# Head attention of a decoder: key chunks in three rounded passes, spread queries fetched in two halves

## The chip, the cores and the metric

The kernel runs on one core of one Trainium2 chip. The metric is the device time of one execution in microseconds. The engines are TensorE (PE, whose weight loads are shown as PEld), VectorE (DVE), ScalarE (ACT) and GpSimd (POOL); SyncE (SP) issues the DMAs.

## What is computed

A decoder of two layers over 32 batches of 56 tokens of width 128. Each layer has a self-attention, a cross-attention on a context of 1500 rows a batch, and a mixture of experts. The part that matters here is the cross-attention of the second layer, with 16 heads of width 8:

```python
def _L1_xattn_ref(query, key, value, Wq, bq, Wk, bk, Wv, bv, Wo, bo):
    q = proj(query, Wq, bq)      # x @ W.T + b, split into 16 heads
    k = proj(key, Wk, bk)
    v = proj(value, Wv, bv)
    scores = jnp.einsum('bhqd,bhkd->bhqk', q, k) / jnp.sqrt(jnp.float32(D_K))
    attn = jax.nn.softmax(scores, axis=-1)
    ctx = jnp.einsum('bhqk,bhkd->bhqd', attn, v)
    ctx = ctx.transpose(0, 2, 1, 3).reshape(B, Sq, D_MODEL)
    return ctx @ Wo.T + bo
...
x = x + _L1_xattn_ref(_layernorm(x, axis=-1), ctx_1024, ctx_1024, ...)
```

## The kernel before

The program runs seven stages one after the other; `head_attention` (from line 1490) is the sixth. Activations are held transposed, channels on partitions. The context of batch p, transposed to 128x1500, comes by one DMA into `ct[u]`, u = p mod 2 (`load`, line 1539).

For each batch the stage makes:

- **Keys.** Three chunks of 500 columns, each one f32 matmul of `HWkT` with a chunk of `ct` into bank 7 (`some_keys`, line 1644). ACT adds the bias and writes `kf` (`copy_keys`, line 1741); GpSimd rounds it to `kh` (line 1799) and subtracts for the remainder `kl` (line 1801), both in the rounded type fp32r. Twelve DMAs (line 1567) place `kh`, `kl`, `kh` below one another in `k3`.
- **Values.** Twelve tiles in three groups of four, f32 (`values`, line 1634), copied to `vs` by ACT (line 1735).
- **Peaks.** 21 matmuls in the rounded type (`peak`, line 1604), numbered m = 0 to 20, into banks 4 and 5 in turn. DVE takes each one's maximum (line 1853). Matmul m waits for maximum m - 2. The maxima's own maximum is turned by TensorE (line 1688) and written to row 96 and on of `q3` (line 1869), as the softmax's shift.
- **Scores.** Twelve tiles t of 125 keys (`score`, line 1623), from `k3` and `q3`; the latter is spread by GpSimd out of `qs` (line 1785, four instructions), which holds the queries and their remainders. ACT takes each tile's exponential (line 1728). Score t waits for exponential t - 2.
- **Weighing.** Twelve tiles of f32 matmuls (`weigh`, line 1614) sum the weighted values in bank 6. DVE picks the sums (`pick`, lines 1825 to 1830), TensorE sums the weights (lines 1589 and 1590), ACT makes the inverse by a logarithm and an exponential (`invert`, lines 1721 and 1723), and DVE multiplies (`divide`, line 1836, whose inputs `on` and `rc` both lie in SBUF).

A slot p holds keys of batch p, peaks and values of p - 1, scores of p - 2, the last four weighings and the pick of p - 3, and the inverse and the divide of p - 4. Every engine has its own written list for a slot, in three rounds i = 0, 1, 2, and works through it strictly in order; semaphores (`Flow.wait`) tie the lists together. `staged` (line 1880) writes slots 0 to 3 out, runs slots 4 to 31 in a loop of two at a time, with addresses in registers, and writes slots 32 and 33 out. In round 0 the lists run:

- TensorE: peak 0, score 0, peak 1, score 1, peak 2, sum of weights, peak 3, weighings 8 to 11 of p - 3, peak 4, score 2, peak 5, values 0, peak 6, score 3, peak 7, values 1.
- ACT: exponentials 0 and 1, `invert`, exponential 2, values, exponential 3, values.
- DVE: maxima 0 to 3, `divide`, `pick`, maxima 4 to 7.
- GpSimd: the spreading of the queries, then `qm` (line 1790, needed by the next slot's peaks), then the rounding of each key chunk as it comes.

In round 1 come scores 4 to 7, peaks 8 to 15, values 2 and, after peak 14, key chunk 0; in round 2 scores 8 to 11, peaks 16 to 20, key chunk 1 after peak 18, the turned maxima, and key chunk 2 between scores 10 and 11. At the start of the stage `spread_queries` (line 1551) fetches all 32 batches' queries into `qs` with 12 DMAs, in SyncE's list before the keys of slot 1. GpSimd waits with the first spreading for all of them.

Of the kernel before, what the change touches and what calls it, by code (L numbers as in the profile page):

```python
# [14 lines left out]
NT = B * L  # L15
# [1474 lines left out]
def head_attention(g):  # L1490
# [13 lines left out]
    with ExitStack() as ctx:  # L1504
# [4 lines left out]
        kf, kl = sb("kf", [128, S]), sb("kl", [128, S], F32R)  # L1509
        kh = [sb(f"kh{u}", [128, S], F32R) for u in range(2)]  # L1510
# [3 lines left out]
        qs = sb("qs", [96, G, NT])  # L1514
# [26 lines left out]
        with nc.Block() as block:  # L1541
            @block.sync
            def _(sp):
                def spread_queries():
                    for n, part in enumerate((g.xn, g.xn, ql)):
# [7 lines left out]
                def slot(p, u, h, keys, maxima, sums):  # L1553
# [17 lines left out]
                staged(sp, B, slot)  # L1571

            @block.tensor
            def _(pe):
# [71 lines left out]
                def slot(p, u, h, keys, maxima, sums):  # L1646
# [56 lines left out]
                staged(pe, B, slot)  # L1703
# [7 lines left out]
            def _(act):  # L1711
                give(act, v_copied, k_full, exped, logged, inverted)
# [24 lines left out]

                def copy_keys(p, n):
# [4 lines left out]
                def slot(p, u, h, keys, maxima, sums):  # L1743
# [21 lines left out]
                staged(act, B, slot)  # L1765
# [4 lines left out]
            def _(pool):  # L1770
                give(pool, q_spread, qm_made, k_high, k_low)
# [6 lines left out]
                def slot(p, u, h, keys, maxima, sums):  # L1778
# [459 lines left out]
```

## Time and profile before

| | us |
|---|---|
| time, median of 3 runs | 1679.98 (1679.1 to 1684.31) |
| time of the profiled execution | 1683.96 |
| its span | 1682.2 |
| head attention in it | about 687 to 1451 |
| TensorE busy, whole span | 1544.6 (92%) |
| DVE busy | 1129.9 (67%) |
| ACT busy | 881.1 (52%) |
| GpSimd busy | 726.3 (43%) |

Times in the trace are microseconds from the start of the span; L1604 is line 1604. A row of the timeline merges instructions of one line that follow each other closely: it shows the first start, the time to the last end and the count. Matmuls are pipelined: the distance from one start to the next tells what one costs, not its recorded duration. The f32 matmuls have two records each.

### The profile page before, as it was taken

The page shows a single profiled execution, that of the slowest core. Times are in us where ns is not written, and L with a number is a line of the kernel's source. Part 1 is how long each engine was busy: PE and PEld are TensorE (multiplying, and loading weights), DVE is VectorE, ACT ScalarE, POOL GpSimd, SP SyncE. Part 2 cuts the span into 40 slices and gives each one's busy share as a digit, 9 for nine tenths or more (in the row PEclk, how much of TensorE's full clock was granted, in tenths as well). Part 3 has the DMA queues.
Part 4 walks back from the last instruction along what each step waited for, and adds up shares of the span by engine and source line. Part 5 has one row for each costly group of instructions (what it writes and reads, how often), then busy time and mean ns, then how long its engine had stood idle before and what let it go on. Part 6 is the DMA issues. An engine that isn't in the chain of part 4 may idle for free. (4 is left out here: it accounts for less than half of the span.)

```text
span 1682.2 us, 45110 instructions
## 1 busy us (share of the span) xinstructions
PE 1544.6 (92%) x16354; PEld 1198.6 (71%) x16354; DVE 1129.9 (67%) x1760; ACT 881.1 (52%) x1387; POOL 726.3 (43%) x786
## 2 busy tenths in 40 slices
PE   7988999899999867679999999999999999889997
PEld 3544766689999545357777777777777777578886
DVE  3643555667887467467777777777777777267877
ACT  4453332432222345436666666666666666566664
POOL 0200000577877444534444433444444333267775
PEclk8988999999999888789999999999999999989999
DMA  2018994131100000286555556665555565112211
GB/s 74 1 34 208 261 255 123 39 124 63 52 30 23 0 2 1 70 180 142 135 132 133 130 137 146 146 146 128 133 132 132 132 146 110 39 36 70 69 56 44
DMA packets 53115, 168.83 MB, mean 100 GB/s; under 512 B 12592, under 2 KB 24720, under 8 KB 53040
## 3 DMA queue, kind: packets, MB, share of 16 engines
q1 hardware_dynamic: 50880, 156.30, 37.2%
q10 hardware_dynamic: 2160, 11.52, 2.4%
q8 instruction: 48, 0.79, 0.2%
q14 instruction: 27, 0.22, 0.0%
HBM read 90.27 MB, written 1.03 MB: 54 GB/s over the span
## 5 line engine op out<-in xcount | busy, mean ns | idle before, releaser
L1853 DVE TENSOR_REDUCE hat_tops<-banks 128x1 f32<-128x500 f32 x672 | 441.7, 677 | 157.9 <-PE banks L1604 156.5
L1728 ACT ACTIVATE hat_pb<-banks 125x896 f32<-125x896 f32 x384 | 340.2, 916 | 226.0 <-PE banks L1623 221.6
L1604 PE MATMUL banks<-hat_kh,hat_qm 128*128 128x500 f32 x672 | 299.4, 463 | 8.2 <-issue 4.8
L1623 PEld LDWEIGHTS banks<-hat_q,hat_k 128*125 128x125 f32 x1536 | 220.3, 189 | 70.9 <-ACT hat_pb L1728 31.9
L1623 PE MATMUL banks<-hat_q,hat_k 128*125 128x224 f32 x1536 | 250.9, 286 | 12.8 <-ACT hat_pb L1728 9.2
L1799 POOL CAST hat_kh<-hat_kf 128x500 fp32r<-128x500 f32 x96 | 58.6, 610 | 391.5 <-DMA hat_k<-hat_kh 303.6
L1614 PE MATMUL banks<-hat_pb,hat_vs 125*27 125x168 f32 (+1 forms) x6144 | 166.9, 261 | 0.1
L1614 PEld LDWEIGHTS banks<-hat_pb,hat_vs 125*27 125x27 f32 (+1 forms) x6144 | 132.0, 98 | 44.1 <-issue 24.4
L1604 PEld LDWEIGHTS banks<-hat_kh,hat_qm 128*128 128x128 f32 x672 | 128.7, 193 | 45.0 <-DVE hat_tops L1853 25.4
L1186 ACT ACTIVATE ffn_rg<-banks 128x448 f32<-128x448 f32 x128 | 69.9, 546 | 162.6 <-PE banks L1120 162.4
L2091 DVE TENSOR_TENSOR moe_hl<-moe_hf,moe_hh 128x448 fp32r<-128x448 f32 x128 | 121.3, 981 | 37.3 <-POOL moe_hh L1982 32.2
L2068 ACT ACTIVATE moe_hf<-banks,moe_b 128x448 f32<-128x448 f32 x144 | 91.6, 637 | 66.1 <-PE banks L2008 55.0
L1801 POOL TENSOR_TENSOR hat_kl<-hat_kf,hat_kh 128x500 fp32r<-128x500 f32 x96 | 120.7, 1257 | 7.7
L1091 POOL CAST ffn_hh<-ffn_hf 128x448 fp32r<-128x448 f32 x112 | 91.1, 813 | 51.4 <-DVE ffn_hf L1232 51.4
L1232 DVE TENSOR_TENSOR ffn_hf<-ffn_rg,banks 128x448 f32<-128x448 f32 x128 | 78.9, 617 | 47.5 <-ACT ffn_rg L1186 45.8
L1634 PE MATMUL banks<-w_HWvT,hat_ct 128*125 128x128 f32 x768 | 103.6, 279 | 0.1
L1634 PEld LDWEIGHTS banks<-w_HWvT,hat_ct 128*125 128x125 f32 x768 | 98.3, 191 | 7.1 <-ACT hat_vs L1735 2.9
L894 POOL CAST ffn_wh<-ffn_raw 128x512 fp32r<-128x512 f32 x24 | 15.4, 641 | 203.9 <-DMA ffn_raw<-FWdT 203.9
L1118 PE MATMUL banks<-n_xh,ffn_wh 128*128 128x448 f32 x256 | 95.0, 371 | 7.3 <-DVE ffn_hf L1232 5.7
L1644 PE MATMUL banks<-hat_ct,w_HWkT 128*128 128x500 f32 x192 | 97.0, 587 | 3.7 <-ACT hat_kf L1741 3.7
L1203 DVE TENSOR_TENSOR ffn_hl<-ffn_hf,ffn_hh 128x448 fp32r<-128x448 f32 x113 | 92.2, 816 | 4.2 <-POOL ffn_hh L1091 4.2
L1120 PE MATMUL banks<-n_xl,ffn_wh 128*128 128x448 f32 x256 | 93.6, 366 | 0.0
(280 smaller groups left out, 3088.7 us busy)
## 6 DMA issues: line engine op xcount, KB each, us to landing
hat_k<-hat_kh SPq DMA_DIRECT2D x256, 187.5 KB, 4.8
hat_ct<-ctxT SPq DMA_DIRECT2D x32, 750.0 KB, 6.1
hat_k<-hat_kl SPq DMA_DIRECT2D x128, 187.5 KB, 4.4
ctx_cx<-ctx SPq DMA_DIRECT2D x32, 672.0 KB
ctx_cd<-ctxT ACTq DMA_DIRECT2D x15, 750.0 KB, 5.9
ffn_cb<-expert_weights SPq DMA_DIRECT2D x8, 896.0 KB, 4.4
moe_cb<-expert_weights SPq DMA_DIRECT2D x8, 896.0 KB, 6.5
moe_raw<-Mw SPq DMA_DIRECT2D x18, 256.0 KB, 3.0
```

The lines of the kernel that those rows point to most:

```text
L1118: nc.tensor.matmul(out, a_high, b_high, start=start, stop=False, skip_group_check=True)
L1120: return nc.tensor.matmul(out, a_high, b_low, start=False, stop=stop, skip_group_check=True)
L1203: low.inc(v.tensor_tensor(hl[:, j % 4, :], hf[:, j % 4, :], hh[:, j % 4, :].bitcast(F32), ALU.subtract))
L1604: peak_out.inc(nc.tensor.matmul(g.bank(PK + m % 2)[:, 0:SB], qm[u][:].rearrange("p h i -> p (h i)")[:, r * 128:r * 128 + 128], kh[u][:, c ...
L1614: mm = nc.tensor.matmul(g.bank(PV)[32 * j:32 * j + V9 * w, n * L:(n + w) * L], vs[u][:, t, HG * j + n:HG * j + n + w, :].rearrange("p h e ...
L1623: mm = nc.tensor.matmul(g.bank(2 * (t % 2) + j // 2)[0:SW, (j % 2) * QW:(j % 2 + 1) * QW], k3[u][:, j, t * SW:(t + 1) * SW], q3[u][:, j, : ...
L1634: mm = nc.tensor.matmul(g.bank(MISC)[0:SW, (i % 4) * D:(i % 4 + 1) * D], ct[u][:, i * SW:(i + 1) * SW], g.w["HWvT"][:], start=True, stop=True)
L1644: k_out.inc(nc.tensor.matmul(g.bank(MISC)[:, 0:SB], g.w["HWkT"][:], ct[u][:, n * SB:(n + 1) * SB], start=True, stop=True))
L1728: exped.inc(nc.scalar.activation(pb[t % 6][:].rearrange("p (n i) -> p n i", n=2), g.ps[0:SW, 2 * (t % 2):2 * (t % 2) + 2, 0:2 * QW], ACT.E ...
L1801: k_low.inc(nc.gpsimd.tensor_tensor(kl[:, cols], kf[:, cols], kh[u][:, cols].bitcast(F32), ALU.subtract))
L1853: peaked.inc(v.tensor_reduce(tops[:, r, n:n + 1], g.bank(PK + m % 2)[:, 0:SB], AX_X, ALU.max))
L2091: low.inc(v.tensor_tensor(hl[:, j % 8, :], hf[:, j % 8, :], hh[:, j % 8, :].bitcast(F32), ALU.subtract))
```

## The change

- Each key chunk becomes three matmuls in the rounded type, which add up in the same bank: high weights with high context, low weights with high context, high weights with low context.
- The weights are split once, at the start of the stage: ACT copies the high part to `kwh`, GpSimd subtracts for `kwl`.
- The context is split in every slot, three chunks of 500 columns: ACT copies (`round_context`) to `cth`, GpSimd subtracts for `ctl`. In ACT's list chunk 0 lies between exponentials 0 and 1, chunk 1 between exponential 1 and `invert`, chunk 2 between exponentials 4 and 5. In GpSimd's list the three subtractions lie between the spreading of the queries and `qm`. `round_context` waits for the context's load, which TensorE's key matmul did before.
- `qs` holds 16 batches in place of 32. The 12 DMAs are issued twice, with half the bytes: in slot 1 and in slot 16, there after the keys' DMAs and once the spreading of batch 15 is done. GpSimd waits for the second set in slot 17.
- `staged_halves` takes the place of `staged` in this stage: slots 4 to 15 in a loop, 16 to 19 written out, 20 to 31 in a loop. In the second half the column in `qs` is counted from batch 16 (`late`).

```diff
@@ tiles
+        cth, ctl = sb("cth", [128, S], F32R), sb("ctl", [128, S], F32R)
+        kwh, kwl = sb("kwh", [128, 128], F32R), sb("kwl", [128, 128], F32R)
+        c_high, c_low = flow("c_high", 3), flow("c_low", 3)
-        qs = sb("qs", [96, G, NT])
+        qs = sb("qs", [96, G, NT // 2])
@@ SyncE
-                def spread_queries():
+                def spread_queries(half):
+                    cols = slice(half * (NT // 2), (half + 1) * (NT // 2))
...
-                            sp.dma_start(qs[32 * n:32 * n + 32, j, :], part[32 * j:32 * j + 32, :]).then_inc(q_in, 16)
+                            sp.dma_start(qs[32 * n:32 * n + 32, j, :], part[32 * j:32 * j + 32, cols]).then_inc(q_in, 16)
...
                     if isinstance(p, int) and p == 1:
-                        spread_queries()
+                        spread_queries(0)
...
+                    if isinstance(p, int) and p == B // 2:
+                        q_spread.wait(sp, p - 1)
+                        spread_queries(1)
@@ TensorE
                 def some_keys(p, u, h, n):
                     if n == 0:
-                        pe.wait_ge(loaded[u], 16 * h + 16)
                         v_copied.wait(pe, p - 1)
+                        if isinstance(p, int) and p == 0:
+                            pe.wait_ge(kw_low, 1)
                     else:
                         k_full.wait(pe, p, n)
-                    k_out.inc(nc.tensor.matmul(g.bank(MISC)[:, 0:SB], g.w["HWkT"][:], ct[u][:, n * SB:(n + 1) * SB], start=True, stop=True))
+                    c_low.wait(pe, p, n + 1)
+                    cols = slice(n * SB, (n + 1) * SB)
+                    nc.tensor.matmul(g.bank(MISC)[:, 0:SB], kwh[:], cth[:, cols], start=True, stop=False)
+                    nc.tensor.matmul(g.bank(MISC)[:, 0:SB], kwl[:], cth[:, cols], start=False, stop=False)
+                    k_out.inc(nc.tensor.matmul(g.bank(MISC)[:, 0:SB], kwh[:], ctl[:, cols], start=False, stop=True))
@@ ACT
+                nc.scalar.copy(kwh[:], g.w["HWkT"][:]).then_inc(kw_high, 1)
...
+                def round_context(p, u, h, n):
+                    if n == 0:
+                        act.wait_ge(loaded[u], 16 * h + 16)
+                    k_out.wait(act, p - 1, n + 1)
+                    cols = slice(n * SB, (n + 1) * SB)
+                    c_high.inc(nc.scalar.copy(cth[:, cols], ct[u][:, cols]))
...
                     for i in range(IT):
                         if sums:
                             exponential(p - 2, 4 * i)
+                        if i == 0 and keys:
+                            round_context(p, u, h, 0)
+                        if i == 1 and keys:
+                            round_context(p, u, h, 2)
+                        if sums:
                             exponential(p - 2, 4 * i + 1)
+                        if i == 0 and keys:
+                            round_context(p, u, h, 1)
                         if i == 0 and reached(p, 4):
                             invert(p - 4)
@@ GpSimd
+                pool.wait_ge(kw_high, 1)
+                nc.gpsimd.tensor_tensor(kwl[:], g.w["HWkT"][:], kwh[:].bitcast(F32), ALU.subtract).then_inc(kw_low, 1)
...
+                        if isinstance(p, int) and p == B // 2 + 1:
+                            pool.wait_ge(q_in, 24 * 16)
...
                     if keys:
+                        for n in range(3):
+                            cols = slice(n * SB, (n + 1) * SB)
+                            c_high.wait(pool, p, n + 1)
+                            c_low.inc(nc.gpsimd.tensor_tensor(ctl[:, cols], ct[u][:, cols], cth[:, cols].bitcast(F32), ALU.subtract))
                         peak_out.wait(pool, p - 2)
                         qm_made.inc(nc.gpsimd.tensor_tensor(qm[u][:], ...
@@ the order of the slots
+def staged_halves(engine, n, slot):
+    for p in range(4):
+        slot(p, p % 2, p // 2, True, p >= 1, p >= 2)
+    with engine.Fori(0, n // 4 - 2) as turn:
+        slot(turn * 2 + 4, 0, turn + 2, True, True, True)
+        slot(turn * 2 + 5, 1, turn + 2, True, True, True)
+    for p in (n // 2, n // 2 + 1, n // 2 + 2, n // 2 + 3):
+        slot(p, p % 2, p // 2, True, True, True, p > n // 2)
+    with engine.Fori(0, n // 4 - 2) as turn:
+        slot(turn * 2 + (n // 2 + 4), 0, turn + (n // 4 + 2), True, True, True, True)
+        slot(turn * 2 + (n // 2 + 5), 1, turn + (n // 4 + 2), True, True, True, True)
+    slot(n, 0, n // 2, False, True, True, True)
+    slot(n + 1, 1, n // 2, False, False, True, True)
```

## Rows read from the trace of the kernel before

**Rows 1.** Windows: length; busy PE, PEld, DVE, ACT, POOL; PEclk, DMA share, GB/s.

```profile
...
770.00:1400.00 630.00, 620.09 (x8390) 492.37 (x8390) 474.83 (x759) 412.25 (x562) 260.90 (x308) 1.00 0.59 138
...
```

**Rows 2.** Timeline, ACT, slots 31 and 32: start, duration, instruction, idle before.

```profile
...
1387.14 2.62 ACT L1728 ACTIVATE hat_pb<-banks 125x896 f32<-125x896 f32 x3
...
1389.95 0.30 ACT L1723 ACTIVATE hat_rc<-hat_rc 128x112 f32<-128x112 f32 x1
...
1400.61 0.92 ACT L1728 ACTIVATE hat_pb<-banks 125x896 f32<-125x896 f32 x1 [2.39 <-PE banks L1623]
...
1408.08 0.92 ACT L1728 ACTIVATE hat_pb<-banks 125x896 f32<-125x896 f32 x1 [2.29 <-PE banks L1623]
1408.92 0.68 ACT L1741 ACTIVATE hat_kf<-banks,w_Hbk 128x500 f32<-128x500 f32 x1
1409.50 2.61 ACT L1728 ACTIVATE hat_pb<-banks 125x896 f32<-125x896 f32 x3
...
```

**Rows 3.** Timeline, TensorE, same columns, slots 31 and 32.

```profile
...
1393.10 0.48 PE L1604 MATMUL banks<-hat_kh,hat_qm 128*128 128x500 f32 x1
...
1400.41 0.39 PE L1604 MATMUL banks<-hat_kh,hat_qm 128*128 128x500 f32 x1
...
1401.70 0.59 PE L1623 MATMUL banks<-hat_q,hat_k 128*125 128x224 f32 x4
...
1403.84 0.40 PE L1604 MATMUL banks<-hat_kh,hat_qm 128*128 128x500 f32 x1
...
1405.46 1.74 PE L1614 MATMUL banks<-hat_pb,hat_vs 125*27 125x168 f32 x64
...
1425.73 0.62 PE L1604 MATMUL banks<-hat_kh,hat_qm 128*128 128x500 f32 x2
...
1427.31 1.74 PE L1614 MATMUL banks<-hat_pb,hat_vs 125*27 125x168 f32 x64
...
```

**Rows 4.** Timeline, DVE, slots 31 and 32.

```profile
...
1390.46 1.10 DVE L1836 TENSOR_TENSOR spare<-hat_on,hat_rc 128x112 f32 x1
...
1392.30 2.65 DVE L1853 TENSOR_REDUCE hat_tops<-banks 128x1 f32<-128x500 f32 x4
...
1412.81 0.59 DVE L1836 TENSOR_TENSOR spare<-hat_on,hat_rc 128x112 f32<-128x112 f32 x1
...
```

**Rows 5.** Timeline, TensorE, expert stage, two passes in a row.

```profile
...
1565.39 0.37 PE L2007 MATMUL banks<-moe_hh,moe_wl 128*128 128x448 f32 x1
1565.59 0.37 PE L2008 MATMUL banks<-moe_hl,moe_wh 128*128 128x448 f32 x1
...
```

**Rows 6.** Source view, line 1716: min/median/max ns, first and last start.

```profile
...
L1716 ACT CAST spare<-xn x4: 564/564/565, 705.7 to 707.5; 128x448 fp32r<-128x448 f32 x4
...
```

**Rows 7.** Timeline, GpSimd, slots 31 and 32, single spreadings among them.

```profile
...
1388.10 1.26 POOL L1801 TENSOR_TENSOR hat_kl<-hat_kf,hat_kh 128x500 fp32r<-128x500 f32 x1
...
1390.87 0.56 POOL L1785 TENSOR_TENSOR hat_q<-hat_qs,constants 96x224 fp32r<-96x224 f32 x1
1391.39 1.72 POOL L1790 TENSOR_TENSOR hat_qm<-xn,constants 128x896 fp32r<-128x896 f32 x1
1402.75 0.60 POOL L1799 CAST hat_kh<-hat_kf 128x500 fp32r<-128x500 f32 x1 [9.64 <-DMA hat_k<-hat_kh]
...
1412.70 0.56 POOL L1785 TENSOR_TENSOR hat_q<-hat_qs,constants 96x224 fp32r<-96x224 f32 x1
...
```

**Rows 8.** Timeline, GpSimd and DVE, start of the stage.

```profile
...
707.59 1.94 POOL L1790 TENSOR_TENSOR hat_qm<-xn,constants 128x896 fp32r<-128x896 f32 x1 [8.38 <-issue]
...
707.90 2.11 DVE L1821 TENSOR_TENSOR spare<-xn,spare 128x448 f32<-128x448 f32 x1
...
```

**Rows 9.** Timeline, TensorE, start of slot 2.

```profile
...
735.95 0.76 PE L1604 MATMUL banks<-hat_kh,hat_qm 128*128 128x500 f32 x1 [4.78 <-issue]
...
```

**Rows 10.** SyncE: key DMAs, slot 31; line 1539, context loads, us to landing.

```profile
...
1395.00 2.79 SPq L1567 DMA_DIRECT2D hat_k<-hat_kh  x4
...
DMA to landing us min/median/max: 4.3/6.1/9.3
...
```

More of the change, by code:

```diff
@@ L1509, in head_attention @@
         kf, kl = sb("kf", [128, S]), sb("kl", [128, S], F32R)
+        cth, ctl = sb("cth", [128, S], F32R), sb("ctl", [128, S], F32R)
+        kwh, kwl = sb("kwh", [128, 128], F32R), sb("kwl", [128, 128], F32R)
+        c_high, c_low = flow("c_high", 3), flow("c_low", 3)
+        kw_high, kw_low = sem("kw_high"), sem("kw_low")
         kh = [sb(f"kh{u}", [128, S], F32R) for u in range(2)]
@@ L1550, in spread_queries, with slot @@
                         for j in range(G):
-                            sp.dma_start(qs[32 * n:32 * n + 32, j, :], part[32 * j:32 * j + 32, :]).then_inc(q_in, 16)
-                def slot(p, u, h, keys, maxima, sums):
+                            sp.dma_start(qs[32 * n:32 * n + 32, j, :], part[32 * j:32 * j + 32, cols]).then_inc(q_in, 16)
+                def slot(p, u, h, keys, maxima, sums, late=False):
                     if keys and (not isinstance(p, int) or p >= 2):
@@ L1639, in some_keys, with slot @@
                     if n == 0:
-                        pe.wait_ge(loaded[u], 16 * h + 16)
                         v_copied.wait(pe, p - 1)
+                        if isinstance(p, int) and p == 0:
+                            pe.wait_ge(kw_low, 1)
                     else:
                         k_full.wait(pe, p, n)
-                    k_out.inc(nc.tensor.matmul(g.bank(MISC)[:, 0:SB], g.w["HWkT"][:], ct[u][:, n * SB:(n + 1) * SB], start=True, stop=True))
-                def slot(p, u, h, keys, maxima, sums):
+                    c_low.wait(pe, p, n + 1)
[3 more added lines that the diff above has]
+                    k_out.inc(nc.tensor.matmul(g.bank(MISC)[:, 0:SB], kwh[:], ctl[:, cols], start=False, stop=True))
+                def slot(p, u, h, keys, maxima, sums, late=False):
                     for i in range(IT):
@@ L1702, in _ @@
                 pe.wait_ge(norm.logged, CH)
-                staged(pe, B, slot)
+                staged_halves(pe, B, slot)
                 for t in range(ST - 4, ST):
@@ L1711, in _ @@
             def _(act):
-                give(act, v_copied, k_full, exped, logged, inverted)
+                give(act, v_copied, k_full, exped, logged, inverted, c_high)
+                nc.scalar.copy(kwh[:], g.w["HWkT"][:]).then_inc(kw_high, 1)
                 norm.on_act(act)
@@ L1741, in copy_keys, with slot @@
                     k_full.inc(nc.scalar.activation(kf[:, n * SB:(n + 1) * SB], g.bank(MISC)[:, 0:SB], ACT.Identity, bias=g.w["Hbk"][:, 0:1]))
-                def slot(p, u, h, keys, maxima, sums):
+                def slot(p, u, h, keys, maxima, sums, late=False):
                     for i in range(IT):
@@ L1763, in slot @@
                             copy_values(p - 1, 1 - u, 1)
-                staged(act, B, slot)
+                staged_halves(act, B, slot)
                 invert(B - 2)
@@ L1770, in _ @@
             def _(pool):
-                give(pool, q_spread, qm_made, k_high, k_low)
+                give(pool, q_spread, qm_made, k_high, k_low, c_low)
+                pool.wait_ge(kw_high, 1)
+                nc.gpsimd.tensor_tensor(kwl[:], g.w["HWkT"][:], kwh[:].bitcast(F32), ALU.subtract).then_inc(kw_low, 1)
+                pool.wait_ge(kw_low, 1)
                 for u in range(2):
@@ L1776, in _, with slot @@
                 pool.wait_ge(q_full, CH)
-                def slot(p, u, h, keys, maxima, sums):
+                def slot(p, u, h, keys, maxima, sums, late=False):
                     if maxima:
@@ L1801, in slot @@
                             k_low.inc(nc.gpsimd.tensor_tensor(kl[:, cols], kf[:, cols], kh[u][:, cols].bitcast(F32), ALU.subtract))
-                staged(pool, B, slot)
+                staged_halves(pool, B, slot)
             @block.vector
@@ L1834, in divide @@
                         dve.wait_ge(q_in, 12 * 16)
+                    if isinstance(q, int) and q == B // 2 - 2:
+                        dve.wait_ge(q_in, 24 * 16)
                     inverted.wait(dve, q)
@@ L1838, in _, with slot @@
                 give(dve, peaked, topped, shifted, own, picked, normed)
-                def slot(p, u, h, keys, maxima, sums):
+                def slot(p, u, h, keys, maxima, sums, late=False):
                     for i in range(IT):
@@ L1871, in slot @@
                                                     spread(c_["own_chunk"][96:96 + ROWS, 0:ROWS], 2, 128), ALU.mult))
-                staged(dve, B, slot)
+                staged_halves(dve, B, slot)
                 divide(B - 2)
```

4 lines of the change are left out of this document (2 added, 2 removed).

## The prediction

> **What bounds the kernel now.** I began with the page's busy shares, then took the window view of the stretch that the change touches, the steady part of the head attention. From 770 to 1400 us TensorE (PE) is busy 620.09 of 630 us at a granted clock of 1.00, DVE 474.83, ACT 412.25 and GpSimd (POOL) 260.90 [rows 1]. So PE sets the pace and each other engine is idle a quarter of the time or more. Idle time, though, is only useful where it lies, so I laid out one slot (one batch's turn of the pipeline) engine by engine. I count from the start of the exponential of tile 11 on ACT, the last of slot 30, at 1387.14 us, into slot 31; the next one is at 1409.50 [rows 2], so a slot is 22.36 us. There are 28 slots with the full set of work (4 to 31).
>
> Two chains run through the first quarter of a slot. PE goes through its own list and reaches the peak matmul of piece 6 at 1393.10, that is 5.96 us in [rows 3]. Meanwhile ACT runs exponentials 11, 0 and 1 and the two steps of `invert`; the second starts at 1389.95 and ends 3.11 us in [rows 2]. DVE holds `divide` and `pick` before the maximum of piece 4: the divide runs 3.32 to 4.42 us in, and the maxima of pieces 4 to 7 start at 5.16 [rows 4]. Piece 6 shares a bank with piece 4, so PE may not start it before maximum 4 is done: 5.16 plus a fourth of 2.65, 5.82. PE arrives at 5.96. The slack of the ACT, DVE, PE chain is 0.14 us at most, and the semaphore's way takes part of that. This is the place that decides.
>
> **What the change takes from PE.** A key chunk is one f32 matmul of 500 columns. From the peak at 1400.41 to score 7 at 1401.70 is 1.29 us and holds the chunk and two peaks [rows 3]. Three rounded passes are of the kind in the expert stage, where 448 columns take 0.20 us from start to start [rows 5]; for 500 columns I estimate 0.22, so 0.66 for a chunk. The f32 chunk takes 1.29 less the two peaks, single passes of 500 columns as well, at 0.22 to 0.23: 0.83 at least. That is 0.17 saved for each of 96 chunks, if nothing else stands behind it.
> Chunk 0: nothing does. All 0.17 counts.
> Chunk 1: from peak 18 (1403.84) to the weighing (1405.46) is 1.62 us. Slot 32 has no chunk there at all, and the same stretch, 1425.73 to 1427.31, still takes 1.58 [rows 3]: peak 20 has to wait for a DVE maximum. Only 0.04 counts.
> Chunk 2: it feeds `copy_keys` at 1408.92, which starts as exponential 10 (from 1408.08) lets ACT go, 0.84 later; exponential 11 then follows at 1409.50 [rows 2]. ACT's own chain sets this stretch. Nothing counts.
> So PE gains 0.21 us a slot, not 0.51.
>
> **What it puts on ACT.** Three copies SBUF to SBUF, 128x500. The nearest row is the cast of the queries, 128x448, at 564 ns [rows 6]; by the exponential's 0.92 us for 896 columns, 52 columns more add some 0.05 [rows 2], so 0.61 recorded. ACT instructions in a row overlap: three exponentials take 2.62 where three times 0.92 would be 2.76. I take 0.52 on the engine; bounds 0.50 and 0.66. The copy of chunk 2 lies between exponentials 4 and 5, ahead of an idle stretch of ACT of 2.39 us, before 1400.61 [rows 2]: free. The copies of chunks 0 and 1 lie between exponentials 0 and 1 and between exponential 1 and `invert`. Behind them are queued `invert`, and on DVE, in order, `divide`, `pick` and every maximum from 4 on. They push the end of `invert` from 3.11 to 4.15.
>
> **What it puts on GpSimd, and where that meets DVE.** Three subtractions of 128x500 at the price of `kl`, 1.26 us: 3.8 us a slot, in a queue that idles 9.64 us before it casts the next keys [rows 7]. The first two come right behind the query spreading, at 4.25 us in, where the 1.72 us `qm` is now; the third waits for the copy of chunk 2, near 11 us in, and pushes `qm` behind it, done near 14. The next keys come 15.6 us in [rows 7], so no late `kh`. GpSimd's time is hidden.
> But a DVE instruction with two inputs in SBUF waits while a GpSimd instruction with SBUF inputs runs. In the start of the stage, `ql` (DVE, two SBUF inputs) starts 707.90 and lasts 2.11 us, to 710.01, while `qm` on GpSimd runs 707.59 to 709.53 [rows 8]: it did its work, about 0.48 us, after GpSimd had ended. `divide` is such an instruction. In slot 32, where its address is fixed, it starts 1412.81 [rows 4], under a spreading of 1412.70 to 1413.26 [rows 7], and ends 1413.40, 0.14 behind that. In slot 31, where the address is in a register, it starts 1390.46 and lasts 1.10 to 1391.56, and loses to the spreading under which it starts and to the next too, which runs 1390.87 to 1391.43 [rows 4, 7]: again it ends 0.13 behind. So its 1.10 us is waiting, and a form with a register asks for the port more than 0.4 us after its start.
> In the new kernel `divide` starts at 3.14 (0.03 behind the end of `invert`, were DVE free) + 1.04 = 4.18 us in. By 4.6, when it asks, GpSimd is in the first new subtraction, 4.25 to 5.51. The divide then ends at 5.51 + 0.13 = 5.64, where it ended at 4.42: 1.22 later, of which 1.04 would come from ACT with a free port and the rest from GpSimd.
> The Trainium skill has a rule for this (SBUF — State Buffer, SBUF: two separate sides): GpSimd and a DVE instruction with two SBUF inputs share one pair of ports under an exclusive lock, and whichever starts first keeps it for its whole instruction. That there is a lock, the trace shows by the numbers above. Read literally, the rule lets a divide in right behind the spreading under which it starts, which is rival 2 below (1675 us); the fixed address does that in slot 32, the register form in slot 31 does not, and there the measurement decides.
>
> **The slot.** PE waits at peak 6 for 1.22 less a slack of 0 to 0.14: 1.15. Later it has no slack of its own to give back (its stretch to exponential 10 is its own work but for what I named). Per slot: 1.15 - 0.21 = +0.94. This holds in the slots whose divide has a register: 4 to 15 and 20 to 31, 24 slots, +22.6. In slots 16 to 19, now written out, the address is fixed; the divide asks at 4.2, before the last spreading ends at 4.29, and ends at 4.43 as before: -0.2 each. Slots 2 and 3 have no divide: -0.2 each. Together -1.2.
>
> **Queries in two halves.** At the start, PE waits 4.78 us at 735.95 for GpSimd, which waits for the DMAs of the first keys [rows 9]. In slot 0 the keys now wait for the rounding of the queries, then two engines, and `qm` behind the subtractions: some 3.7 us later by the same prices. That fits in the 4.78, and half as many query bytes ahead of the keys in the queue helps. Bounds -3 and +4, taken +0.5. In slot 16 SyncE issues 12 more DMAs behind the 12 of the keys, at the present 0.70 (four in 2.79), 8.4 us [rows 10]. The load of the next context, which now follows the keys' DMAs at 10.65 us in, goes at 19 and lands 6.1 us later, at 25.1 [rows 10]; ACT will need it at 24.05 (22.36, and two exponentials of 0.845 before its first copy). +1, bounds 0 and +4.
>
> **The sum.** 22.6 - 1.2 + 0.5 + 1 = +22.9 us. The profiled execution took 1683.96 us around a span of 1682.2, the median of the three runs is 1679.98; an increase in one stage carries over: 1679.98 + 22.9 = 1702.9, say 1703.
>
> **Rivals.** (1) The full gain: nothing stands behind the chunks and the copies are hidden: 96 x 0.17 = 16 us off, 1664. Slot 32 and the slack of 0.14 speak against it. 0.03.
> (2) The divide gets the port as soon as it starts, at 4.2, before the last spreading ends, and PE only gains: 30 x -0.21 + 1.5, 1675. For it: it misses by 0.1 us only; against: in all 28 slots the register form lost. 0.12.
> (3) The divide stays 1.10 long: late by 1.04 - 0.18 = 0.86, PE +0.58 a slot, 24 x 0.58 - 1.2 + 1.5, 1694. 0.17.
> (4) It loses to the second subtraction as well, 1.22 later still: 24 x 2.16 - 1.2 + 1.5, 1732. 0.06.
> (5) The passes aren't quicker: then the slot is +1.15, 1709; the expert rows speak against it. 0.02.
> The forecast has 0.60. Its own range is 1697 to 1711, by the bounds of the start, the fetch and the slack; (3) with the same bounds reaches down to 1687. The range 1683 to 1716 holds these two and (5), 0.79 in all, and leaves out (1), (2) and (4).
> A measurement here can tell 0.3%, 5 us. It lies at 1675, so (2) falls half to either side of it. Faster: (1) and half of (2), 0.09, taken 0.10. Same: the rest of (2) and the low end of (3), 0.10. Slower: 0.80.
>
> **What would show it.** Each key chunk as three PE records 0.21 to 0.23 apart; copies on ACT of 0.61; PE idle of 1.0 to 1.2 us before peak 6, released by DVE's maximum; `divide` starting about 0.9 later than now and ending 0.13 behind a GpSimd subtraction, 1.4 to 1.5 us long; slots of 23.3 us in the loops and 22.2 in the four written out. It is wrong if `divide` ends before 4.5 us in, or if ACT's copies take 0.3.

## The result and the profile after

The changed kernel takes 1701.06 us, the median of four runs (1697.68 to 1713.6), against 1679.76 before. The ratio is 1.0129, 95% interval 1.0089 to 1.0169. Measured again beside the later experiments it was 1.0106 (1.0065 to 1.0148). Every ratio below is to runs of the kernel before taken beside that experiment, with its 95% interval in brackets. The forecast of 1703 is a ratio of 1.0137. The profiled execution took 1698.69 us around a span of 1696.9, 14.7 us over that of before.

Lines of the kernel after have other numbers: L1612 is `peak`, L1622 `weigh`, L1631 `score`, L1655 to L1657 the three passes, L1735 and L1737 `invert`, L1742 `exponential`, L1757 `round_context`, L1762 `copy_keys`, L1818 the spreading of the queries, L1825 the subtraction of the context, L1827 `qm`, L1875 `divide`, L1892 the maxima. In the experiments' kernels they lie a few lines off; the tiles' names tell them apart. First the busy times on the page of the kernel after, then its windows view, 770 to 1400 us, with the columns of [rows 1]:

```profile
...
PE 1533.4 (90%) x16450; PEld 1217.1 (72%) x16450; DVE 1134.3 (67%) x1760; ACT 921.5 (54%) x1484; POOL 843.5 (50%) x883
...
770.00:1400.00 630.00, 595.23 (x8182) 494.49 (x8181) 467.74 (x734) 432.95 (x625) 354.69 (x382) 1.00 0.58 135
...
```

TensorE is busy 595.23 us of 630, where it was 620.09, so it is idle 34.8 us in place of 9.9 while fewer slots pass: it waits. The waits view of the same stretch (who waited for whom; total, times, longest) has the two ends of the chain that it waits for, TensorE behind DVE's maximum and DVE's divide behind ACT:

```profile
...
PE banks L1612 <- DVE hat_tops L1892: 22.0, 27, 0.8
...
DVE spare L1875 <- ACT hat_rc L1737: 23.6, 27, 0.9
...
```

Neither pair had as much as a line of this kind before. One slot in full, in the order of the forecast: ACT, then DVE and GpSimd, then TensorE. Exponential 11 starts at 1400.52 and is the zero of the counts below.

```profile
...
1399.15 0.92 ACT L1742 ACTIVATE hat_pb<-banks 125x896 f32<-125x896 f32 x1 [2.41 <-PE banks L1631]
1399.96 0.67 ACT L1762 ACTIVATE hat_kf<-banks,w_Hbk 128x500 f32<-128x500 f32 x1
1400.52 1.73 ACT L1742 ACTIVATE hat_pb<-banks 125x896 f32<-125x896 f32 x2
1402.11 0.63 ACT L1757 CAST hat_cth<-hat_ct 128x500 fp32r<-128x500 f32 x1
1402.61 0.95 ACT L1742 ACTIVATE hat_pb<-banks 125x896 f32<-125x896 f32 x1
1403.42 0.63 ACT L1757 CAST hat_cth<-hat_ct 128x500 fp32r<-128x500 f32 x1
...
1404.25 0.30 ACT L1737 ACTIVATE hat_rc<-hat_rc 128x112 f32<-128x112 f32 x1
...
```

```profile
...
1404.69 1.47 DVE L1875 TENSOR_TENSOR spare<-hat_on,hat_rc 128x112 f32 x1 [0.88 <-ACT hat_rc L1737]
...
1406.83 2.61 DVE L1892 TENSOR_REDUCE hat_tops<-banks 128x1 f32<-128x500 f32 x4
...
```

```profile
...
1404.25 0.57 POOL L1818 TENSOR_TENSOR hat_q<-hat_qs,constants 96x224 fp32r<-96x224 f32 x1
...
1404.76 1.27 POOL L1825 TENSOR_TENSOR hat_ctl<-hat_ct,hat_cth 128x500 fp32r<-128x500 f32 x1
...
```

```profile
...
1391.66 0.40 PE L1612 MATMUL banks<-hat_kh,hat_qm 128*128 128x500 f32 x1
1391.90 0.39 PE L1655 MATMUL banks<-hat_cth,hat_kwh 128*128 128x500 f32 x1
1392.12 0.39 PE L1656 MATMUL banks<-hat_cth,hat_kwl 128*128 128x500 f32 x1
1392.35 0.39 PE L1657 MATMUL banks<-hat_ctl,hat_kwh 128*128 128x500 f32 x1
1392.57 0.39 PE L1612 MATMUL banks<-hat_kh,hat_qm 128*128 128x500 f32 x1
1392.80 0.59 PE L1631 MATMUL banks<-hat_q,hat_k 128*125 128x224 f32 x4
...
1394.94 0.40 PE L1612 MATMUL banks<-hat_kh,hat_qm 128*128 128x500 f32 x1
...
1396.53 1.74 PE L1622 MATMUL banks<-hat_pb,hat_vs 125*27 125x168 f32 x64
...
1407.55 0.50 PE L1612 MATMUL banks<-hat_kh,hat_qm 128*128 128x500 f32 x1 [0.82 <-DVE hat_tops L1892]
...
```

The copies are recorded at 0.63 us and take 0.50 of the engine (1402.11 to 1402.61, 1403.42 to 1403.92). `invert` ends 4.03 us in, `divide` starts at 4.17 and ends at 5.64, 0.13 behind the subtraction that ran 1404.76 to 1406.03. The maxima of pieces 4 to 7 start at 6.31, and peak 6 comes at 7.03, after a wait of 0.82; it came at 5.96 before [rows 3], so it is 1.07 later. The passes stand 0.22 to 0.23 apart. From one divide to the next it is 23.17 us in the mean, against 22.39.

### The profile page after: what moved, and what is told of

Read it like the earlier page. It is cut to its first block and busy times, and to the rows that moved or that the text cites. A ratio compares the mean times of both kernels' runs of the same rounds, so it can differ in the third digit from the quotient of the medians.

```text
span 1696.9 us, 45133 instructions
## 1 busy us (share of the span) xinstructions
PE 1533.4 (90%) x16450; PEld 1217.1 (72%) x16450; DVE 1134.3 (67%) x1760; ACT 921.5 (54%) x1484; POOL 843.5 (50%) x883
## 5 line engine op out<-in xcount | busy, mean ns | idle before, releaser
L1892 DVE TENSOR_REDUCE hat_tops<-banks 128x1 f32<-128x500 f32 x672 | 442.3, 677 | 142.9 <-PE banks L1612 142.6
L1742 ACT ACTIVATE hat_pb<-banks 125x896 f32<-125x896 f32 x384 | 345.4, 921 | 214.2 <-PE banks L1631 211.0
L1612 PE MATMUL banks<-hat_kh,hat_qm 128*128 128x500 f32 x672 | 277.9, 430 | 26.1 <-DVE hat_tops L1892 25.8
L1631 PEld LDWEIGHTS banks<-hat_q,hat_k 128*125 128x125 f32 x1536 | 217.7, 187 | 56.8 <-ACT hat_pb L1742 35.5
L1631 PE MATMUL banks<-hat_q,hat_k 128*125 128x224 f32 x1536 | 237.7, 277 | 16.8 <-ACT hat_pb L1742 12.8
L1825 POOL TENSOR_TENSOR hat_ctl<-hat_ct,hat_cth 128x500 fp32r<-128x500 f32 x96 | 120.5, 1268 | 141.6 <-ACT hat_cth L1757 141.6
L1622 PE MATMUL banks<-hat_pb,hat_vs 125*27 125x168 f32 (+1 forms) x6144 | 166.9, 261 | 0.1
L1612 PEld LDWEIGHTS banks<-hat_kh,hat_qm 128*128 128x128 f32 x672 | 127.7, 192 | 53.7 <-DVE hat_tops L1892 44.8
L1622 PEld LDWEIGHTS banks<-hat_pb,hat_vs 125*27 125x27 f32 (+1 forms) x6144 | 132.4, 98 | 42.8 <-issue 23.4
L1232 DVE TENSOR_TENSOR ffn_hf<-ffn_rg,banks 128x448 f32<-128x448 f32 x128 | 79.0, 618 | 49.5 <-ACT ffn_rg L1186 48.6
```

Source lines behind the costliest of these rows:

```text
L1612: peak_out.inc(nc.tensor.matmul(g.bank(PK + m % 2)[:, 0:SB], qm[u][:].rearrange("p h i -> p (h i)")[:, r * 128:r * 128 + 128], kh[u][:, c ...
L1622: mm = nc.tensor.matmul(g.bank(PV)[32 * j:32 * j + V9 * w, n * L:(n + w) * L], vs[u][:, t, HG * j + n:HG * j + n + w, :].rearrange("p h e ...
L1631: mm = nc.tensor.matmul(g.bank(2 * (t % 2) + j // 2)[0:SW, (j % 2) * QW:(j % 2 + 1) * QW], k3[u][:, j, t * SW:(t + 1) * SW], q3[u][:, j, : ...
L1742: exped.inc(nc.scalar.activation(pb[t % 6][:].rearrange("p (n i) -> p n i", n=2), g.ps[0:SW, 2 * (t % 2):2 * (t % 2) + 2, 0:2 * QW], ACT.E ...
L1825: c_low.inc(nc.gpsimd.tensor_tensor(ctl[:, cols], ct[u][:, cols], cth[:, cols].bitcast(F32), ALU.subtract))
L1892: peaked.inc(v.tensor_reduce(tops[:, r, n:n + 1], g.bank(PK + m % 2)[:, 0:SB], AX_X, ALU.max))
```

## Where the time went

From the issue of the stage's first context load to its last divide (starts read from the timelines; the period is the mean distance between divides of slots 4 to 31, the length the usual one in the loops):

| kernel | stage, us | against before | load to first divide | period | length of divide |
|---|---|---|---|---|---|
| before | 763.53 | | 98.66 | 22.39 | 1.10 |
| after | 781.59 | +18.1 | 95.84 | 23.17 | 1.45 |
| after, second time | 782.74 | +19.2 | 97.02 | 23.17 | 1.45 |
| `invert` first | 752.74 | -10.8 | 94.29 | 22.16 | 0.57 |
| subtractions wait | 753.34 | -10.2 | 95.00 | 22.19 | 0.28 |
| no subtractions | 755.19 | -8.3 | 95.67 | 22.22 | 0.28 |
| halves only | 754.89 | -8.6 | 90.20 | 22.39 | 1.10 |
| second subtraction waits | 753.68 | -9.9 | 95.02 | 22.20 | 0.28 |
| `qm` waits (before) | 761.54 | -2.0 | 96.68 | 22.39 | 0.58 |
| copies only | 759.75 | -3.8 | 93.95 | 22.44 | 0.28 |
| `qm` ahead | 850.55 | +87.0 | 96.25 | 25.65 | 3.10 |

The other stages differ by up to 15 us from one profile to the next for all kernels alike (that first load is issued anywhere between 679.41 and 693.95 us), so the table is better than the spans for small parts. The time from load to first divide scatters too: 95.84 and 97.02 us for the same source, 98.66 and 96.69 for before and `qm` waits, which run the same instructions up to there. Differences of 1 to 2 us in that column mean little. +18.1 us in 1680 is 1.0108, within both intervals.

## The experiments

**The order on ACT.** `e1_invert_first`:

```diff
                         if sums:
                             exponential(p - 2, 4 * i)
-                        if i == 0 and keys:
-                            round_context(p, u, h, 0)
...
                             exponential(p - 2, 4 * i + 1)
-                        if i == 0 and keys:
-                            round_context(p, u, h, 1)
                         if i == 0 and reached(p, 4):
                             invert(p - 4)
+                        if i == 0 and keys:
+                            round_context(p, u, h, 0)
+                            round_context(p, u, h, 1)
```

> The changed kernel with one thing moved: on ACT the copies of context chunks 0 and 1 come behind `invert` in place of around exponential 1. The same instructions run on every engine. Theory (the divide is late, first by ACT's copies and then by GpSimd's subtraction): `divide` starts 3.3 us after exponential 11 again, ends at 4.4 behind the last spreading (length 1.10), no TensorE wait at peak 6, and TensorE keeps what the three passes save: slots of 22.1 us against 22.39 before and 23.16 in the changed kernel; total about 1668, ratio to before 0.993. Rival A (the load on ACT or on GpSimd as such costs, wherever it lies): slots stay at 23.2, total 1697 to 1701. Rival B (three passes cost TensorE more than they save): slots of 22.4 or more, total 1676 or more.

Measured 1672.94 us, ratio 0.9953 (0.9932 to 0.9974), slots of 22.16. The same work on every engine, two copies moved behind `invert`, and the loss is a gain: in the slots neither the load on ACT or GpSimd nor the passes cost the time. It beats the kernel before, and the changed one by 1.5%. One number was off: the divide was 0.57 long, not 1.10. GpSimd and DVE of one slot (single spreadings, then the divide):

```profile
...
1194.63 0.56 POOL L1817 TENSOR_TENSOR hat_q<-hat_qs,constants 96x224 fp32r<-96x224 f32 x1
...
1195.15 0.59 POOL L1817 TENSOR_TENSOR hat_q<-hat_qs,constants 96x224 fp32r<-96x224 f32 x1
...
1194.74 0.58 DVE L1874 TENSOR_TENSOR spare<-hat_on,hat_rc 128x112 f32 x1
...
```

It starts under the third spreading, as in [rows 4] and [rows 7], but ends behind the third and not behind the fourth, in the loop, with its address in a register. My explanation of the 1.10, that a form with a register asks for the port late, could not be right.

**The order on GpSimd.** `e2_divide_before_low`:

```diff
                     if keys:
+                        if reached(p, 4):
+                            normed.wait(pool, p - 4)
                         for n in range(3):
```

> The changed kernel with one wait more: GpSimd starts the three context subtractions of slot p only when `divide` of p - 4 is done. ACT's order and all work stay. Theory: `divide` starts at 4.2 us as in the changed kernel, but finds no subtraction in its way; it ends between 4.4 and 5.1 (how long the register form takes with a free port no row shows), where it ended at 5.64. Slots between 22.1 and 22.6, total 1668 to 1682. In the four written-out slots (16 to 19) it is at most 0.6 long. Rival A (ACT's copies alone make the delay, the port adds nothing): slots stay at 23.1 to 23.2, total as the changed kernel or, as GpSimd begins later, above it.

Measured 1675.2 us, ratio 0.9967 (0.9941 to 0.9994), slots of 22.19. The divide is 0.28 long in the register form: it costs no more than the fixed one. ACT still ends `invert` a microsecond late, and with the port free that costs the slots nothing. The refetch shows here: in slot 17 ACT waits 0.86 us for the context load, and that slot is 23.11 long, 0.9 more than the usual one. The same slot is 23.97 long in the next run, where ACT waits 1.71.

**No subtractions.** `e3_no_low_context`; the low part of the context is left out of the keys:

```diff
-                        for n in range(3):
-                            cols = slice(n * SB, (n + 1) * SB)
-                            c_high.wait(pool, p, n + 1)
-                            c_low.inc(nc.gpsimd.tensor_tensor(ctl[:, cols], ct[u][:, cols], ...
...
-                    c_low.wait(pe, p, n + 1)
+                    c_high.wait(pe, p, n + 1)
```

> The changed kernel without the subtractions of the context: `ctl` is set to zero once, so the third pass adds nothing. The passes and ACT's copies stay; GpSimd has 3.8 us a slot less to do, and `qm` (1.70 us) stands again right behind the spreading. Theory (a divide that starts at 4.2 waits for whichever GpSimd instruction runs next): it waits for `qm`, to 4.25 + 1.70 + 0.13 = 6.1 in place of 5.64, length 1.9. With less work the slot grows, to 23.5 or 23.6; total 28 x 0.4 above the changed kernel less 1 to 3 at the start, 1707 to 1710. Rival (GpSimd's load as such costs): slots fall below 23.16, to 22.4 if it is the whole cost, total 1675 to 1697.

Measured 1673.61 us, ratio 0.9942 (0.9917 to 0.9967): a miss of over 30 us. The divide did not wait for `qm` at all:

```profile
...
1184.54 0.56 POOL L1820 TENSOR_TENSOR hat_q<-hat_qs,constants 96x224 fp32r<-96x224 f32 x1
...
1185.05 1.77 POOL L1825 TENSOR_TENSOR hat_qm<-xn,constants 128x896 fp32r<-128x896 f32 x1
...
1185.00 0.28 DVE L1873 TENSOR_TENSOR spare<-hat_on,hat_rc 128x112 f32 x1 [0.90 <-ACT hat_rc L1737]
...
```

The divide starts at 1185.00, under a spreading that ends at 1185.10, and ends at 1185.28; `qm`, started at 1185.05 by the record, took 1.77 in place of 1.70. So it went ahead of `qm`, though in the changed kernel the divide at the same place did not go ahead of the subtraction. The rival of this run, load on GpSimd, names the right number but not the right reason: `invert` first and the run before this one carry all the load and are as fast.

**The second part alone.** `e4_halves_only`: the changed kernel with `some_keys` as before and without `round_context`, the splitting of the weights and the subtractions.

```diff
-                    c_low.wait(pe, p, n + 1)
-                    nc.tensor.matmul(g.bank(MISC)[:, 0:SB], kwh[:], cth[:, cols], start=True, stop=False)
-                    nc.tensor.matmul(g.bank(MISC)[:, 0:SB], kwl[:], cth[:, cols], start=False, stop=False)
-                    k_out.inc(nc.tensor.matmul(g.bank(MISC)[:, 0:SB], kwh[:], ctl[:, cols], start=False, stop=True))
+                    k_out.inc(nc.tensor.matmul(g.bank(MISC)[:, 0:SB], g.w["HWkT"][:], ct[u][:, n * SB:(n + 1) * SB], start=True, stop=True))
```

> The kernel before with the second part of the change alone: queries fetched in two halves and the slots written as two loops with four written out between; keys in f32, no rounding of the context. Theory: slots 4 to 31 stay at 22.39, also where the second half is fetched, and only the start of the stage gets shorter, by the wait for the first keys' DMAs (4.8 us before): total 3 to 6 us below before, ratio 0.997. Rival A (the halves cost: a second fetch delays a context load, code of four more slots is fetched): total 0 to 5 above before. Rival B (the start gains nothing): same as before within 0.1%.

Measured 1676.88 us, ratio 0.9961 (0.9938 to 0.9983). The slots stay at 22.39 and the start is 8.5 us shorter, more than the wait of 4.78 us [rows 9]. The windows view, 724 to 748 us, of before and then of this kernel (granted clock: third number from the end), and behind it peak 0 of slot 2 in this kernel (its timeline of TensorE):

```profile
...
724.00:748.00 24.00, 16.90 (x69) 12.52 (x69) 12.78 (x21) 7.92 (x11) 12.93 (x16) 0.72 0.72 162
...
```

```profile
...
724.00:748.00 24.00, 20.78 (x165) 14.77 (x166) 18.91 (x30) 11.01 (x15) 9.17 (x11) 1.00 0.76 172
...
733.86 0.78 PE L1612 MATMUL banks<-hat_kh,hat_qm 128*128 128x500 f32 x1
...
```

Peak 0 of slot 2 comes 43.43 us after the stage's first load (issued at 690.43), where it was 48.76 (735.95 [rows 9] less 687.19): 5.3 of the 8.5 us, about the wait. The rest, 3.1 us, comes with the clock. Before, the granted clock in this stretch was 0.72 and TensorE worked 16.90 us of 24; here it is 1.00, the full level of 2.4 GHz, and 20.78 (the stage began 3.24 us later here, so the two stretches are not quite the same place of it). In the kernel before it is 0.50, the level of 1.2 GHz, from 731.65 to 745.20, across the wait and 9 us behind it. A third run bears this out: `e7_before_qm_waits` below runs the same instructions as before up to the first divide, has the wait too (4.18 us), but only some 6 us of the lower clock behind it. From peak 0 of slot 2 to the first divide it takes 48.6 us, between the 49.9 of before and the 46.8 here. The four slots written out show the fixed form of the divide at 1.09 and 1.10, like the register form.

The pure counterpart, the passes without the halves, was not run, so what the passes do at the start is seen only together with the halves.

**What the divide waits for.** Laid side by side, the runs have this in common. At the moment the divide starts, let GpSimd have a run of instructions: the one that it is in, and those behind it that are ready then. Before: spreadings 3 and 4, `qm`; the divide gets in ahead of `qm`. After: spreading 4, subtractions 1 and 2; it gets in ahead of subtraction 2. No subtractions: spreading 4, `qm`; ahead of `qm`. `invert` first: spreadings 3 and 4, since subtraction 1 isn't ready yet (ACT's copy for it ends some 0.3 us after the divide has started); ahead of spreading 4. Each time it is the last of the run. Two kernels test that against "the next one holds the port".

`e5_second_low_waits`:

```diff
                             c_high.wait(pool, p, n + 1)
+                            if n == 1 and reached(p, 4):
+                                normed.wait(pool, p - 4)
```

> The changed kernel with one wait: only the second of GpSimd's three context subtractions waits for `divide` of p - 4; the first still runs right behind the spreading. The traces so far fit a pattern: a divide that comes while GpSimd runs X loses to the next instruction Y if the one behind it, Z, is ready too, and gets in ahead of Y if Z isn't. Theory P (that pattern): Z now waits for the divide, so the divide gets in ahead of the first subtraction: 0.28 to 0.4 long, no TensorE wait at peak 6, slots of 22.15, total 1668 to 1676 and a ratio near that of the wait before all three subtractions (0.997). Theory N (whatever runs next on GpSimd holds the port): the divide is still 1.45 long, slots of 23.16, total as the changed kernel, ratio 1.008 to 1.013.

Measured 1676.79 us, ratio 0.9964 (0.9937 to 0.9991), slots of 22.20. All the work, all the load, and the first subtraction next in line at the same instant:

```profile
...
1184.41 0.55 POOL L1818 TENSOR_TENSOR hat_q<-hat_qs,constants 96x224 fp32r<-96x224 f32 x1
...
1184.93 1.32 POOL L1827 TENSOR_TENSOR hat_ctl<-hat_ct,hat_cth 128x500 fp32r<-128x500 f32 x1
...
1184.86 0.27 DVE L1877 TENSOR_TENSOR spare<-hat_on,hat_rc 128x112 f32 x1 [0.91 <-ACT hat_rc L1737]
...
```

The divide goes ahead of it, 0.27 long; the subtraction takes 1.32 in place of 1.27. The refetch costs its slot 1 us here too (23.18). What held the port in the changed kernel was not the first subtraction as such but that a second one was ready behind it.

`e6_qm_ahead`: `qm` before the three subtractions.

```diff
                     if keys:
+                        peak_out.wait(pool, p - 2)
+                        qm_made.inc(...)
                         for n in range(3):
...
-                        peak_out.wait(pool, p - 2)
-                        qm_made.inc(...)
```

> The changed kernel with `qm` (1.70 us) ahead of the three context subtractions on GpSimd; all else the same. Theory P: X is the last spreading, Y is `qm`, Z the first subtraction, ready: the divide loses to `qm` and is 1.85 to 1.9 long, though in the run without subtractions it went ahead of the same `qm`; slots of 23.16 + 0.44 = 23.6, total about 1705 to 1712, ratio 1.017 to 1.021. Rival M (`qm` never holds the divide up, subtractions do, by what they read or write): the divide is 0.28 long, slots of 22.2, ratio 0.996. The key chunks wait for GpSimd 1.7 us longer; chunk 0 has some 5 us of room, so neither theory counts that.

Measured 1770.34 us, ratio 1.0518 (1.0469 to 1.0567). The divide loses to `qm`, which it overtook above, and then to subtraction 1 too:

```profile
...
1199.61 0.55 POOL L1818 TENSOR_TENSOR hat_q<-hat_qs,constants 96x224 fp32r<-96x224 f32 x1
...
1200.13 1.68 POOL L1823 TENSOR_TENSOR hat_qm<-xn,constants 128x896 fp32r<-128x896 f32 x1
...
1201.78 1.23 POOL L1827 TENSOR_TENSOR hat_ctl<-hat_ct,hat_cth 128x500 fp32r<-128x500 f32 x1
...
1200.06 3.08 DVE L1875 TENSOR_TENSOR spare<-hat_on,hat_rc 128x112 f32 x1 [0.91 <-ACT hat_rc L1737]
...
```

It starts at 1200.06 and ends at 1203.14, 0.13 behind subtraction 1 and ahead of subtraction 2, the last of the run. That both would pass it I had not counted, a miss of some 60 us; the pattern as first put named only the next instruction. The slots are 24.81 and 26.42, mostly in turn. The first is the 1.6 us that the divide is longer. The other 1.6 of the long slots is the clock. The windows view of a short slot, of the long one behind it and of a part of that (TensorE busy: the second number; granted clock: third from the end):

```profile
...
1200.06:1224.86 24.80, 21.87 (x305) 18.14 (x301) 18.86 (x28) 15.97 (x23) 12.99 (x15) 1.00 0.54 126
1224.86:1251.30 26.44, 23.52 (x308) 19.73 (x301) 18.80 (x28) 15.96 (x23) 13.01 (x15) 0.94 0.51 118
1230.00:1233.50 3.50, 3.50 (x18) 3.33 (x16) 1.79 (x3) 1.50 (x2) 0.00 (x0) 0.51 1.01 206
...
```

TensorE waits for the maximum at peak 6 in both slots, 2.46 and 2.45 us. In the long one the granted clock is at the lower level for 3.5 us right behind the wait, and TensorE is busy 1.65 us longer. Why one wait is followed by it and the next is not, no run shows.

`e7_before_qm_waits`, the kernel before with one wait:

```diff
                     if keys:
+                        if reached(p, 4):
+                            normed.wait(pool, p - 4)
                         peak_out.wait(pool, p - 2)
```

> The kernel before with one wait: GpSimd starts `qm` of slot p only when `divide` of p - 4 is done. Theory P, widened by the last runs (a divide gets in ahead of the last instruction of an unbroken run of ready GpSimd instructions, not earlier): the run is now the four spreadings alone, so the divide gets in ahead of the fourth and is 0.58 long in all slots, where it was 1.10 and got in ahead of `qm`. Register or fixed address makes no difference. The slot stays at 22.39, since the divide's end has 0.14 us or less to give and TensorE sets the pace: time as before within 0.3%. Theory R, which my forecast used (a form with its address in a register asks for the port 0.4 us late): the divide stays 1.10 long in slots 4 to 31.

Measured 1688.01 us, ratio 1.0025 (0.9989 to 1.006), slots of 22.39. The run of spreadings ends with the fourth, and the divide is 0.57 or 0.58 long in every slot of the loop, with its address in a register:

```profile
...
1193.15 0.56 POOL L1785 TENSOR_TENSOR hat_q<-hat_qs,constants 96x224 fp32r<-96x224 f32 x1
...
1193.67 0.59 POOL L1785 TENSOR_TENSOR hat_q<-hat_qs,constants 96x224 fp32r<-96x224 f32 x1
...
1193.27 0.58 DVE L1838 TENSOR_TENSOR spare<-hat_on,hat_rc 128x112 f32 x1
...
```

Half a microsecond less on the divide moves no slot, as TensorE sets the pace there.

**The delay on ACT alone.** `e8_copies_only`: the changed kernel without the subtractions and with the matmul of before; ACT's copies stay.

```diff
-                    c_low.wait(pe, p, n + 1)
+                    c_high.wait(pe, p, n + 1)
...
+                    k_out.inc(nc.tensor.matmul(g.bank(MISC)[:, 0:SB], g.w["HWkT"][:], ct[u][:, n * SB:(n + 1) * SB], start=True, stop=True))
```

> The changed kernel with the keys in f32 again and without the context subtractions; ACT's three copies stay where they are and their result isn't used. Theory P: `invert` ends 1.0 us later, the divide starts at 4.2 and gets in ahead of `qm`, the last of its run: 0.28 long, ended at 4.4 as before. ACT's delay by itself costs nothing: slots of 22.39, a start as in the run with halves alone, ratio 0.996 to 0.997. Theory A (the delay of `invert` costs, at least in part): slots of 22.6 to 23.2, ratio 1.000 or more.

Measured 1676.48 us, ratio 0.9978 (0.9955 to 1.0001), 0.28 for the divide, 22.39 for a slot but for the two behind the refetch (23.34 and 22.89, the late load again). In the second of them the divide starts while `qm`, the last of its run, is under way, and is 1.02 long: it doesn't break into an instruction that runs. In the slots, then, ACT's delay by itself is free. Elsewhere it is not: the start was forecast as with the halves alone and is 3.75 us longer (93.95 against 90.20). The first key matmul comes 21.42 us after the first load, where it came at 17.51 with the halves alone, for it now waits for ACT.

**The changed kernel again**, `a2_changed_again`, the same source:

> The changed kernel itself, for a ratio beside the same runs of before: 28 slots at +0.77 us and a start that is 5 us shorter give +16 to +18 us, ratio 1.010 to 1.011. If the 21 us between the first medians were real, 1.013.

Measured 1702.14 us, ratio 1.0106 (1.0065 to 1.0148).

## Why the prediction was right, and where it was right for a wrong reason

The place, the chain and the length of the divide came out as forecast. Of the reasons behind the number, one failed, and two errors of 4 us that it and the slack made cancel by luck.

- **The place.** Peak 6, behind the chain ACT, `divide`, `pick`, maximum 4, with a slack of 0.14 us. Shown: the wait of 0.82 us there (forecast 1.0 to 1.2), and its end when either ACT's order or GpSimd's is changed (slots of 22.16 and 22.19).
- **What the passes save.** Forecast 0.21 a slot. Chunk 0: from peak to score 1.14 us where it was 1.29, 0.15 (forecast 0.17). Chunk 1: 1.59 from peak 18 to the weighing, where it was 1.62 (forecast 0.04). Chunk 2: exponential 10 to 11 takes 1.37, where it was 1.42; forecast nothing, measured 0.05. With `invert` first the slot is 22.16 against 22.39, 0.23 in all: the idea of three passes is worth 6.4 us, not the 16 of a count of passes.
- **ACT.** Two copies: forecast 1.04 us of delay, measured 0.50 for each copy and 0.92 in the end of `invert` (4.03 against 3.11). The divide starts 0.14 behind that, where I had taken 0.03, so that its start, forecast at 4.18 and measured at 4.17, is in part chance.
- **The divide's end.** Forecast 5.64 us in, measured 5.64. The step behind it failed. I had put the 1.10 us of before down to the register form, which "asks for the port more than 0.4 us after its start". The fixed form was as long at the same place (1.09 and 1.10, halves only), and the register form took 0.57 with `invert` first and 0.28 with a free port. The pair of slots that I had compared differs in one thing more: slot 32 makes no keys, so no `qm` is ready behind its fourth spreading. What decides is how many ready instructions GpSimd has behind the one that runs. The number came out right, by luck, since GpSimd had two subtractions ready, and the divide went between them.
- **The four written-out slots.** This is where the wrong step shows in the forecast: -0.2 us each, measured +0.77 each, for the fixed form waits like the other (1.58 and 1.51). 3.9 us too low.
- **The slots in the loops.** Forecast +0.94, measured +0.77, 24 of them: 4.1 us too high. Peak 6 is 1.07 later and not 1.15; 0.07 more is made up by peak 8 (1.00 later, in the mean of 18 slots of the loops), where I had given TensorE nothing to make up; and the passes save 0.23 and not 0.21. This error and the one before cancel.
- **The start.** Forecast +0.5 with bounds -3 and +4, measured -3.7 (95.84 less the 0.85 that the divide is later in its slot, against 98.66), and -2.5 the second time; slots 2 and 3, which I had counted apart at -0.4, are in it. It has two parts. The halves give -8.5, more than the wait that I named, because the clock granted behind the wait was higher too. The rounding and the two engines ahead of the first keys take 4 to 5 of it back: the first key matmul comes at 23.53 after the first load and not at 17.61, 5.9 later where I had forecast 3.7, and the start with `invert` first is 4.1 longer than with the halves alone. Most of that is there with ACT's copies alone (3.75).
- **The refetch.** Forecast +1: nothing in the changed kernel, where ACT doesn't wait for that load (its slots are 0.77 longer), and 0.9 to 1.8 us in the slot where it shows in the kernels without the port's wait; with `invert` first ACT needs the load later, and it costs nothing either. The size was right, but in the changed kernel the other loss covers it.
- **The sum.** +22.9 forecast, +18.1 in the stage by the traces: 28 slots at 0.77 less 3.7, within 0.2. What is left of the difference, about 5 us, is the start and the refetch. The medians differ by 21.3 us the first time, and the intervals of both ratios contain 1.0108 (+18.1) and 1.0136 (+22.9).
- Of the rivals, (2), where the divide gets the port and the time is about 1675, is what `e2_divide_before_low` and `e5_second_low_waits` measured, at the price of one wait. Rival (4), which loses twice, is the mechanism of `e6_qm_ahead`.

The rule that I quoted from the Trainium skill (SBUF — State Buffer, SBUF: two separate sides) holds here in its first half, the lock: a DVE instruction with two SBUF inputs ended 0.13 us behind a GpSimd instruction wherever it was longer than 0.28 us in the slots shown (0.14 in the kernel before with one wait). Its second half, that whichever starts first keeps the pair, does not hold by the records: in the changed kernel the divide is recorded from 1404.69 and the subtraction from 1404.76, and the subtraction was done first. The divide let one instruction pass behind the one under which it started in the changed kernel, and two in `e6_qm_ahead`.

## What to carry to other kernels

A gain on the engine that sets the pace is worth only what the waits behind it let through: look in each place for what else would be late there, and take a stretch of the same trace without the work as the bound. Small work added to an idle engine belongs behind the step that others wait for, not ahead of it; here moving two copies was worth 28 x 1.0 us, though a microsecond of delay alone cost the slots nothing: it cost where it brought the divide to a place with two long instructions ready on GpSimd. And where GpSimd has a queue of ready instructions, a short DVE instruction with two SBUF inputs can wait for all of them but the last; one wait on GpSimd for that instruction was worth 28 us (753.34 against 781.59).

## What the runs showed of the hardware that I had not expected

- A `divide` of 112 columns takes 0.28 us with a free port, whether its address is fixed or in a register; 0.57, 1.10, 1.45 and 3.08 us are the same instruction behind the rest of one spreading; that and one more spreading; the rest of one and a subtraction; the rest of one, `qm` and a subtraction.
- With a run of GpSimd instructions that are ready when it starts, it gets the port ahead of the last of them (or behind the last, if it starts under that one: 1.02 us in one slot of the copies alone). Six arrangements fit this (before, after, `invert` first, no subtractions, second subtraction waits, `qm` ahead), and the kernel before with one wait and the copies alone were forecast from it. The rule took its present form only after `e6_qm_ahead` had missed. What in the chip makes it so, no run shows.
- At the start of the stage a shorter wait of TensorE was followed by a granted clock of 1.00 in place of 0.72 over 24 us, and the start of the stage was 8.5 us shorter where the wait itself was 4.78.
- Behind waits of 2.45 us of TensorE the granted clock was 0.51 for 3.5 us in about every second slot of `e6_qm_ahead`, which made these slots 1.6 us longer; behind the waits of 0.82 us in the changed kernel it stayed at 1.00.
